# A one-core attention and feed-forward kernel with its table of steps written in another order

## The reference, cut to what matters

```python
def attn(h):                                  # h: layernorm of x
    q = rope((h @ Wq.T).astype(bf16)); k = rope((h @ Wk.T).astype(bf16))
    s = exp(q @ k.T / sqrt(128)), zero above the diagonal
    o = s.sum(axis=-1)                        # one number a row; there is no V
    return relu(o @ fc1_w.T + fc1_b) @ fc2_w.T + fc2_b   # 16 inner values
def ffn(h):                                   # the gates pick expert 1 with weight 1
    return relu(h @ W1[1] + b1[1]) @ W2[1] + b2[1]       # 128 -> 256 -> 128
x = x + layernorm(attn(layernorm(x)))
x = x + layernorm(ffn(layernorm(x)))
```

## Time and profile before

| | before |
|---|---|
| runs, median (lowest to highest) | 92.8 us (92.72 to 94.83), 3 runs |
| profiled execution, its own time | 92.89 us |
| its span in the trace | 91.1 us |
| busy PE, DVE, ACT, POOL | 82.2, 78.9, 67.7, 56.8 us |
| granted TensorE clock, mean | 0.994 |

### The profile page before, as it was taken

The page is one execution under the profiler, slowest core; times in us unless marked ns, Lnnn a source line. Parts: engine busy times, 40 slices in busy tenths (PEclk is TensorE's granted clock), DMA queues, the critical chain, the costliest instruction groups (busy, mean ns, idle before and its releaser), DMA issues.

```text
span 91.1 us, 1515 instructions
## 1 busy us (share of the span) xinstructions
PE 82.2 (90%) x439; PEld 49.2 (54%) x443; DVE 78.9 (87%) x210; ACT 67.7 (74%) x190; POOL 56.8 (62%) x79
## 2 busy tenths in 40 slices
...
GB/s 42 289 256 272 270 179 161 207 146 67 164 11 85 122 23 0 102 17 0 0 0 0 0 0 7 0 0 0 0 7 7 115 0 0 0 0 89 286 262 169
DMA packets 11852, 7.64 MB, mean 84 GB/s; under 512 B 819, under 2 KB 10948, under 8 KB 11844
## 3 DMA queue, kind: packets, MB, share of 16 engines
...
...
## 4 chain that ended last, share of the span: by engine, by line
PE 54%; ACT 23%; SPq 9%; DMA 5%; issue 2%; DVE 1%; POOL 1%; POOLq 1%; DVEq 0%
ACT psum L549 18%; PE psum L719 17%; PE psum L791 15%; PE psum L745 10%; DMA x_s<-x 5%; PE psum L711 5%; SPq L324 4%; PE psum L770 3%; SPq L304 2%; ACT fc L562 1%; PE psum L764 1%; ACT qk L501 1%; ACT h1T L518 1%; PE psum L749 1%; PE psum L781 1%
## 5 line engine op out<-in xcount | busy, mean ns | idle before, releaser
L485 POOL TENSOR_TENSOR rstd<-ve,half_neg 128x4 f32<-128x4 f32 (+1 forms) x36 | 35.7, 997 | 27.9 <-DVE ve L350 17.7
L549 ACT ACTIVATE psum<-psum 128x1024 f32<-128x1024 f32 (+7 forms) x48 | 36.5, 761 | 0.6 <-PE psum L749 0.2
L745 PE MATMUL psum<-qk_r 128*128 128x512 bf16 (+3 forms) x76 | 19.7, 346 | 1.8 <-ACT psum L549 1.3
L719 PE MATMUL psum<-cols_n,wqk 128*128 128x512 f32 (+1 forms) x36 | 16.9, 561 | 0.0
L719 PE MATMUL psum<-cols_n,w_c 128*128 128x512 f32 (+1 forms) x36 | 15.9, 551 | 0.0
L791 PE MATMUL psum<-w_c,hid 128*128 128x128 f32 x128 | 15.8, 276 | 0.0
L791 PEld LDWEIGHTS psum<-w_c,hid 128*128 128x128 f32 x128 | 15.3, 192 | 0.7 <-issue 0.3
L745 PEld LDWEIGHTS psum<-qk_r 128*128 128x128 bf16 x80 | 6.6, 97 | 12.9 <-ACT psum L549 6.3
L501 ACT ACTIVATE cols_n<-psum 128x512 f32<-128x512 f32 (+1 forms) x12 | 6.3, 528 | 8.2 <-PE psum L711 8.2
L711 PE MATMUL psum<-ident,rows_n 128*128 128x128 f32 x64 | 10.1, 276 | 0.9 <-DVE rows_n L344 0.9
L711 PEld LDWEIGHTS psum<-ident,rows_n 128*128 128x128 f32 x64 | 7.4, 141 | 5.9 <-issue 3.3
...
## 6 DMA issues: line engine op xcount, KB each, us to landing
...
```

The source lines that it names most:

```text
L485: ready[k].done(eng.tensor_tensor(rstd[:, g, STAT_SLOT[k], t], ve[:, g, STAT_SLOT[k], t], half_neg[:, 0:tiles], ALU.pow), n)
L549: exps.done(eng.activation(area, area, ACT.Exp, scale=scale_qk, accum_out=sums[:, g, s, j:j + 1]), n, j, s)
L719: made[name].done(eng.matmul(bank_of(name, n)[:, 0:tiles * P], weight, cols_n[:, g, c], start=True, stop=True), n)
L745: mm = eng.matmul(psum[:, own[0] + i, 0:width], query, qk_r[:, g0 + c, 1, 0:width], start=True, stop=c < gb)
```

## The change: the table of steps in another order

All 430 or so words of `STEPS` are there as before, but for: `load_fc` issued by SP instead of ACT, `blank.9`, `blank.1.128`, `blank.1.128` turned into `blank.8`, `blank.1.256`, `blank.1`, `blank.1.256`, and the engine's letter of about 50 words. Nearly every word stands in another place and many PSUM banks are others. The letters that differ: `cos` of units 0, 1, 5, 7 goes from DVE to POOL and `cos.2` the other way; `norm1` of units 5, 6, 8 from POOL to DVE and `norm1.1` from DVE to POOL; `+q` of units 1, 3, 5 from ACT to DVE, `+k.3` from DVE to ACT; `+tr1.2`, `+trz.5`, `+w1` from DVE to ACT and `+tr1.5` the other way; `stat5` of units 2, 3, 4 from DVE to ACT, `stat3` of units 6, 7 and `stat5.7` from ACT to DVE; single `+h0`, `+h1`, `norm4` and `eps` words. A second list `OUTS` gives the units of the last steps; it equals `BACKS`, so it alters nothing by itself. The code for one tile a bank is new, and no word of the table uses it.

```diff
+OUTS = [(0, 0, 4), (1, 0, 4), (4, 0, 4), (5, 0, 4), (2, 0, 4), (6, 0, 4), (3, 0, 4), (7, 0, 2), (7, 2, 2)]
 STEPS = """
-load_x.0 blank.9#7 blank.1.128#7 load_x.3 repeat.0 load_x.4 mask.0 load_fc.0.A load_b1.0 load_wqk.0 stat1.0 load_x.1
+load_x.3 blank.8#6 blank.1.256#6 load_x.4 repeat.0 load_wqk.0 mask.0 load_x.2 load_x.0 stat1.3 load_w1.0 load_b2.0
...
+OUT_STEPS = {"y", "bias", "stat5", "eps5", "rstd5", "ys", "out", "store"}
...
+        back_of = {(g, j): n for n, (g, j0, tiles) in enumerate(BACKS) for j in range(j0, j0 + tiles)}
...
-            g, j0, tiles = (FRONTS if name in FRONT_STEPS else BACKS)[n]
+            g, j0, tiles = (FRONTS if name in FRONT_STEPS else OUTS if name in OUT_STEPS else BACKS)[n]
...
+            if per_bank == 1:
+                return psum[:, own[j]:own[j] + 2, 0:P].rearrange("p t c -> p c t")
...
-                        for i in range(2):
-                            r = slice(PAIR * i, PAIR * (i + 1))
-                            mm = eng.matmul(psum[:, own[i], 0:2 * P], h1T[r, n, :],
-                                            fc2[r, 2 * i:2 * i + 2, :].rearrange("p j c -> p (j c)"), start=True, stop=True)
+                        per_bank = tiles // len(own)
+                        for i, b in enumerate(own):
+                            j = slice(i * per_bank, (i + 1) * per_bank)
+                            r = slice(BLOCK * j.start, BLOCK * j.stop)
+                            mm = eng.matmul(psum[:, b, 0:per_bank * P], h1T[r, n, :],
+                                            fc2[r, j, :].rearrange("p j c -> p (j c)"), start=True, stop=True)
...
-                    taken["h0"].wait(eng, n)
-                    taken["h1"].wait(eng, n)
+                    taken["h0"].wait(eng, back_of[g, j0])
+                    taken["h1"].wait(eng, back_of[g, j0])
```

More of the change, by code:

```diff
@@ L38 @@
 STEPS = """
[L39 to L68, removed]
@@ L74 @@
-+trz.8.A +h0.6.A rstd5.3 ys.4 h1.8#2 +h1.6.A h0.8#7 trz.7#0 out.0.P out.3 +h0.8.A y.6#6 +trz.7.A +h1.8.A out.4.P
-stat5.1.D store.0 store.5 h1.7#2 store.3 eps5.1.D stat5.6.D rstd5.1 h0.7#3 store.4 +h1.7.D y.8#0 eps5.6.A +h0.7.D
-rstd5.6 out.1 y.7#3 stat5.8.A out.6 eps5.8.P store.1 stat5.7.A rstd5.8 eps5.7.D out.8 store.6 rstd5.7 store.8 out.7
-store.7
+load_x.3 blank.8#6 blank.1.256#6 load_x.4 repeat.0 load_wqk.0 mask.0 load_x.2 load_x.0 stat1.3 load_w1.0 load_b2.0
+eps1.3.D stat1.4 rstd1.3 load_x.6 wqk.0#0 load_x.1 eps1.4.A rstd1.4 norm1.3.D load_x.8 blank.1#6 blank.1.256#6
@@ new lines @@
++wqk.0.A load_w2.0 stat1.0 tr1.3#1 norm1.4.D load_table.1 w1.0#0 +tr1.3.A eps1.0.D load_x.5 stat1.2 tr1.4#2 rstd1.0
+b2mean.0 load_fc.0 k.3#1 stat1.6 +tr1.4.A eps1.2.P b2.0 norm1.0.D q.3#3 load_table.0 eps1.6.D stat1.8 w2mean.0 rstd1.6
+load_x.7 k.4#2 stat1.1 eps1.8.A load_table.2 +q.3.D +k.3.A rstd1.8 tr1.0#4 w2.0 norm1.6.D q.4#5 swap.3 +k.4.A rstd1.2
+norm1.8.D tr1.6#3 +q.4.A load_b1.0 cos.3.D fc.0#2 +tr1.6.A swap.4 eps1.1.D stat1.5 norm1.2.P tr1.8#5 +tr1.0.A fcmean.0
+q.6#3 stat1.7 +tr1.8.A load_table.4 rstd1.1 +w1.0.A cos.4.D k.6#4 load_table.3 +q.6.A sin.3.D eps1.5.A k.0#0 +fc.0
```

47 lines of the change are left out of this document (37 added, 10 removed).

## The result

The changed kernel takes **95.5 us** (median of 4 runs, 95.3 to 95.66) against 92.8 us on the same chip: ratio 1.0273, interval 1.0228 to 1.0318. The forecast was 92.0 us with a range to 93.6, so it was wrong, in sign and by 3.5 us. The profiled execution took 95.3 us with a span of 93.5 us.

The account below looks back on a forecast made before the run. PE's list was taken to bound the kernel. Opening +0.3, middle −1.5, end 0 and POOL with DVE +0.4 gave −0.8 us: 92.89 to 92.1 profiled, 92.0 us as median, range 90.5 to 93.6.

Parts of the forecast that it names:

- The opening's blocks: Opening: loads land at one pace, 279 KB a microsecond, no charge for late blocks; whole opening loses 0.3 us.
- The meetings: DVE instructions held up while POOL works on a product, two likely near PE's path: loss 0.4 us.
- The middle: From 17.4 us to PE's last 24.5 us of work: PE's stalls fall from 3.8 to 2.3 us, gain 1.5.
- My sign: PE's idle time between 17 and 60 us at about 1.3 us; wrong if it stays above 2 us.
- my ten times 0.16 us: Middle: some ten PE stalls, each about 0.16 us longer than its idle entry, added to 2.2 us idle.
- my second rival: Middle: PE's stalls go from ACT to DVE and stay about 3.5 us, no gain, 92.8 us; chance 0.22.
- The end: PE's last stretch and the steps behind its last matmul: nothing gained or lost, 0 us.
- slower rival: Opening: DVE stands for a late table with cos.3 in front, POOL's norm1.1 meets rope.3; 94.0 us, chance 0.12.
- its point of 17.4: Opening: the slower case decides from the point where rope.3 ends after 17.4 us.

Follow-up runs that it names:

- the run without a meeting: Changed kernel with eps1.1 and eps1.7 on ACT, norm1.7 and cos.0 on DVE, twelve empty matmuls for eight, load_table.3 before load_table.4: 92.9 us, ratio 0.9995.

## Why the prediction was wrong, step by step

All distances are in the profiled executions. The mark is the point where PE has 24.5 us of work left, the start of `y.0`. The prediction had it at 60.2 us before any charge for meetings (61.4 + 0.3 − 1.5). In the changed kernel it is 64.13 us (59.82 plus 4.31, which the piece from `y.2` on takes in each kernel of this order that I read), 3.9 us late.

- **The opening's blocks (0 charged, 0.8 measured).** The first `k` started at 8.73 us (9.0 predicted). But the statistics of unit 6 waited for their block until 9.75, `norm1.8` came at 13.52, and `cos.3` at 14.13 instead of 13.3. With the same order of loads those statistics began at 9.86 us with twelve blanks and ran at 8.9 us without a wait in the run without a meeting, so this term scatters from one execution to the next; I had taken one pace, 279 KB a microsecond, from one execution. (At that pace 2505 KB are down at 12.8 us, not at the 12.6 that I wrote; `cos.3` did not wait for its table.)
- **The meetings (0.4 charged, 1.6 measured). This is the first step that failed.** `cos.3` to `y.2` takes 45.69 us in the changed kernel (14.13 to 59.82) and 44.05 without a meeting (13.26 to 57.31); with the two `eps` on ACT it is 44.74 (13.88 to 58.62). My bounds, 0 to 2.4 us, held it; the value I took did not. I had looked at products with two inputs only, and guessed `norm1.1` with `rope.3`. In fact what was held were two `eps` of two and four numbers a row, a copy and one norm. (I also had POOL lose two of three `norm1`; it had five and keeps three, and two of these hold a step of DVE.) The four rows are 2.65 us too long; 1.6 reach PE, not half of one as I had put it. The run without a meeting also has twelve blanks and the two tables in the other order, so the 1.6 is not of the meetings alone. The Trainium skill, page "SBUF — State Buffer", section "Who interferes with whom", lists `copy` and `tensor_scalar` beside the products: where their operands allow it, both may enter a mode that takes the ports shared with GpSimd, and whoever comes second then waits for a whole instruction. I had used that page's line on two inputs and left this one out. The rows agree with it: 0.16 against 1.01 us, 0.21 against 1.06.
- **The middle (gain of 1.5 charged, 0.1 measured). The second step that failed.** Without a meeting `cos.3` is at 13.26, as predicted, and the first score row 0.4 us late at 17.76. The mark is at 61.62 us: 1.4 later than my 60.2, of which 0.4 lie ahead of that score row and 1.0 behind it, and no earlier than the 61.4 of the kernel before. My sign was PE's idle time; it is 0.95 us in that execution (22.80 and 21.20 less 22.13 and 20.92, below), less than the 1.3 that I asked for and 1.25 less than before, and yet nothing was won at the mark: the idle entries of PE are no measure of its stalls, and my ten times 0.16 us was no correction for it. From 31 to 45 us the lists of DVE, ACT and PE are level (above), and nothing that I moved shortened the stretch behind `+q.5`. I had taken it that fewer waits of PE shorten the chain, where DVE and ACT had no slack to give. I had also given signals between engines no time, as my second rival said: the waits change their name, 92.8 us. With the meetings taken away, and twelve blanks, that is the result to 0.1 us. How much of the missing gain is signals and how much the full lists is not shown.
- **The end (0 charged, a gain of 0.3).** From the mark to the end of the span it took 29.4 us against 29.7 before; the part behind the last matmul is about as long as it was.

```profile
17.40:40.20 22.80, 22.13 (x111) 10.73 (x110) 22.55 (x51) 22.56 (x60) 9.85 (x11) 1.00 0.26 60
40.20:61.40 21.20, 20.92 (x115) 11.22 (x114) 19.49 (x55) 20.57 (x53) 12.59 (x17) 1.00 0.06 12
```

This is the stretch table of the run without a meeting: against the changed kernel PE does 1.4 us more in the first stretch and ACT 1.6. DVE is at the same 22.55, but of the changed kernel's 22.56 us some 1.8 are the excess of three held rows. Beside the earlier trace rows, DVE and ACT are as full as before the change, and the edits that moved DVE's work to ACT (a norm, two copies) gave nothing or lost.

The sum of the changed kernel in hindsight: 92.1 + 0.8 (blocks) + 1.2 (meetings beyond 0.4) + 1.4 (middle) − 0.3 (end) = 95.2 us, against 95.3 in the profiled execution. The terms were read off that execution and its neighbours, so the agreement is no test. The **slower rival** had the place right, DVE in the opening with the table's product in front and POOL on the other side, and `rope.3` ended at 19.1 us (18.37 + 0.69), past its point of 17.4. It had the wrong partner and the wrong reason, since `eps1.1` was held and not `rope.3`, and the table was there in time. Its price of 94.0 us had the middle without a gain already; it counted one meeting, and three of the four held rows, 1.8 of the 2.65 us, come after `rope.3`. The `fc` loads on SP cost 0.35 to 0.5 us, which the intervals do not tell from zero.

What stays open: whether the 0.8 us of the four blanks is PE's first steps at half pace; what the loads of `b2` and `w2` would be worth with no new meeting; why PE's first steps ran at half their pace in some executions at a granted clock of 1.00 (last section); and whether a different order of `cos` and `norm1` on POOL, clear of every small step of DVE, would beat 92.8 us. No version here beats the kernel before.
